# Two layers with attention on one core: loads of queries, keys and values move from SyncE's to ScalarE's DMA issue

## The chip, the core and the metric

The kernel runs on one core of a Trainium2 chip. A core has five engines with an instruction stream each: TensorE (PE in the profile, with its weight loads apart as PEld), VectorE (DVE), ScalarE (ACT), GpSimd (POOL) and SyncE (SP), which computes nothing and issues transfers. TensorE reads SBUF and writes PSUM. Transfers between DRAM and SBUF are DMAs; an engine issues one with an instruction of its own stream, and 16 DMA engines move the bytes. The engines wait for one another through semaphores only. The metric is the time of one execution on the device in microseconds, and less is better. Three runs of the kernel before gave 1760.53, 1763.01 and 1766.39 us; their median is 1763.01 us.

## The reference

Two layers work on 2 sequences of 1024 tokens with 512 features. Each layer normalizes x, computes a mixing part and a feed-forward part from it and adds both to x. The change touches the attention of the second layer alone:

```python
qkv = x @ W_qkv.T + b_qkv                       # b=2, l=1024, d=512
q, k, v = jnp.split(qkv, 3, axis=-1)            # 16 heads of 32 features
scores = jnp.einsum('bqhe,bkhe->bhqk', q, k) * scale
scores = jnp.where(causal[None, None], scores, -jnp.inf)
attn = jax.nn.softmax(scores, axis=-1)
out = jnp.einsum('bhqk,bkhe->bqhe', attn, v)
out = out.reshape(b, l, d) @ W_out.T + b_out
```

Layer 0 is a low-rank state-space mixer beside a gated feed-forward with a Walsh-Hadamard turn; layer 1 is this attention beside a gated feed-forward that keeps 2 of each 4 hidden values.

## The kernel before

The program is four phases with a barrier of all engines between them: `layer_zero`, `project_qkv`, `attention` and `layer_end`. `project_qkv` parks queries, keys and values in DRAM (`qk_parked`, `v_parked`). Every float32 operand is held as a rounded part and a rest (`hi` and `lo`), and a product is several matmuls.

`attention` takes 32 heads one after the other: 16 heads of the model times 2 sequences. `QUADS` is 4 and `HB` is 8, so a quad is 8 such heads, 4 of sequence 0 and then 4 of sequence 1. The values of one quad and one sequence lie in `v[:, b]` (1040 KB). Queries and keys of two heads (a pair) lie in one of three slots of the tile `stack` or `stack_third`.

The work of a head is this. TensorE computes 8 score blocks of 128 queries (`score`, line 1501). VectorE takes the negated maximum of each row of a block (`top`, line 1575), which gives a column of 128 numbers in `row_top`. A DMA (`place`, line 1473) writes this column as a row into the query slot, so that the second product, `turned` (line 1516), yields the transposed scores with the maximum already subtracted. Places 0 to 3 serve the first 512 queries, places 4 to 7 the second 512, and `turned` 0 and 4 wait until the four places of their half have landed (line 1509). ScalarE takes the exponential (`exp`, line 1547) and rounds it (`round`, line 1555) for 8 of 12 blocks; VectorE subtracts for those (`rest`, line 1582); GpSimd does both steps for the other 4 (`divide`, lines 1595 and 1598). TensorE multiplies by the values (`weigh`, lines 1533 and 1534) into one PSUM bank `p_o`; ScalarE reads it out twice a head (`read_o`, line 1564), which frees the bank, and SyncE stores it (`store`, lines 1480 and 1481).

The order of all this is written out by hand in the table `ORDER`, one list for each engine, which `run` walks for every head h. An entry is a step, its number within the head, and how many heads ahead of h it is. An engine executes its list strictly in this order. SyncE issues every DMA of the program. Within the attention its list holds the places, the stores, the loads of the next pair (`stack`, three DMAs of 256 KB a head, queries for even h and keys for odd h, `load_part`, line 1153) and, once each four heads, the load of values (`values`, line 1158, six of them).

Of the kernel before, what the change touches and what calls it, by code (L numbers as in the profile page):

```python
# [11 lines left out]
F32 = mybir.dt.float32  # L12
# [7 lines left out]
B, S, D = 2, 1024, 512  # L20
# [8 lines left out]
HEADS, E = 16, 32  # L29
# [1116 lines left out]
        load_part(sp, slot, qk_dram, pair, what, stacked)  # L1146


def load_part(sp, slot, qk_dram, pair, what, stacked):
    r = 2 * E * what  # L1150
    for block in range(3):
        half = block // 2 if what == 0 else block % 2
        sp.dma_start(slot[E * block:E * block + E, :, what].bitcast(F32),
                     qk_dram[pair][half, r:r + 2 * E, :].rearrange("(a e) n -> e a n", a=2)).then_inc(stacked, 16)


def load_values(sp, v, v_dram, quad, b, loaded):
    sp.dma_start(v[:, b].rearrange("p t a c -> p (t a c)").bitcast(F32), v_dram[B * quad + b]).then_inc(loaded, 16)


def project_qkv(nc, wqk, wv, masks, x_hi, x_lo, qk_dram, v_dram, stack, v_first, mask, ahead, qk_parts, qk_stored):
# [193 lines left out]
def attention(nc, mask, stack, v, qk_dram, v_dram, o_dram, sum_dram, o_both, o_stored, qk_last, load_next):  # L1355
# [3 lines left out]
    QUADS = HEADS // 4  # L1359
    HB = B * 4  # L1360
    ROWS = QB * G
    BL = 12
# [13 lines left out]
                   ("weigh", 11, 0), ("score", 4, 2), ("turned", 3, 1), ("turned", 4, 1), ("turned", 5, 1)],  # L1376
        "scalar": [("exp", 3, 0), ("exp", 4, 0), ("round", 3, 0), ("exp", 5, 0), ("round", 5, 0), ("read_o", 0, 0),
                   ("exp", 6, 0), ("exp", 7, 0), ("exp", 8, 0), ("round", 7, 0), ("exp", 9, 0), ("exp", 10, 0),
                   ("round", 9, 0), ("exp", 11, 0), ("round", 10, 0), ("round", 11, 0), ("exp", 0, 1),
                   ("round", 0, 1), ("exp", 1, 1), ("exp", 2, 1), ("round", 2, 1), ("read_o", 1, 0)],  # L1380
        "vector": [("top", 4, 1), ("rest", 2, 0), ("rest", 3, 0), ("top", 5, 1), ("rest", 5, 0), ("top", 6, 1),
                   ("rest", 7, 0), ("top", 7, 1), ("top", 0, 2), ("rest", 9, 0), ("top", 1, 2), ("top", 2, 2),
                   ("rest", 10, 0), ("rest", 11, 0), ("rest", 0, 1), ("top", 3, 2)],
        "gpsimd": [("divide", 4, 0), ("divide", 6, 0), ("divide", 8, 0), ("divide", 1, 1)],
        "sync": [("place", 4, 1), ("store", 0, 0), ("values", 0, 0), ("place", 5, 1), ("place", 6, 1), ("place", 7, 1),
                 ("stack", 2, 0), ("place", 0, 2), ("place", 1, 2), ("place", 2, 2), ("place", 3, 2), ("store", 1, 0)],
    }

    with ExitStack() as ctx:
# [9 lines left out]
        slots = [stack[:, 0], stack[:, 1], third[:]]  # L1399

        stacked = [sem(f"stacked{i}") for i in range(3)]
# [8 lines left out]
        def wait(engine, semaphore, count):  # L1410

            if count > 0:
                engine.wait_ge(semaphore, count)
# [28 lines left out]
        def run(steps, order):  # L1442
            for h in range(-AHEAD, HB * QUADS):
                for step, n, ahead in order:
                    if 0 <= h + ahead < HB * QUADS:
                        steps[step](h + ahead, n)
# [2 lines left out]

        @block.sync  # L1450
        def _(sp):
            def next_stack(h, n):
                pair = h // 2 + n
                if pair < HEADS:
                    wait(sp, turned, 2 * BL * (pair - 2))
                    load_part(sp, slots[pair % 3], qk_dram, pair, h % 2, stacked[pair % 3])
                if h == HB * (QUADS - 1):
                    load_next(sp)

            def next_values(h, n):  # L1460
                quad, at = divmod(h, HB)
                if at == 0 and quad:
                    sp.wait_ge(weighted, HB * BL * quad)
                    load_values(sp, v, v_dram, quad, 1, v_loaded[1])
                if at == 4 and quad + 1 < QUADS:
                    sp.wait_ge(weighted, HB * BL * quad + HB * BL // 2)
                    load_values(sp, v, v_dram, quad + 1, 0, v_loaded[0])

            def place(h, r):
                sp.wait_ge(topped, ROWS * h + r + 1)  # L1470
                if r % QB == 0:
                    wait(sp, placed[r // QB], 16 * QB * h)
                sp.dma_start(slot_of(h)[K3:K3 + 1, h % 2, 0, r * P:(r + 1) * P].bitcast(F32),
                             top[:, h % 2, r:r + 1].bitcast(F32)).then_inc(placed[r // QB], 16)

            def store(h, g):
                b, pr, a = place_of(h)
                sp.wait_ge(o_read, G * h + g + 1)
                row, t0, i = E * (2 * pr + a), b * S + g * W, (G * h + g) % OS
                sp.dma_start(o_dram[h // HB, :, row:row + E, t0:t0 + W], o_both[0:2 * E, i]).then_inc(o_stored[i], 16)  # L1480
                sp.dma_start(sum_dram[TT * (h // HB) + G * b + g, row // E:row // E + 1], o_both[2 * E:VC, i])\
                    .then_inc(o_stored[i], 16)

            sp.wait_ge(*qk_last)
            run({"stack": next_stack, "values": next_values, "place": place, "store": store}, ORDER["sync"])

        @block.tensor
        def _(pe):
# [51 lines left out]
        def _(act):  # L1540
# [16 lines left out]
            def read_o(h, g):  # L1557
                act.wait_ge(weighted, BL * h + (BL if g else QB))

                if (h, g) == (0, 0):  # L1560
                    act.wait_ge(*qk_last)
                i = (G * h + g) % OS
                wait(act, o_stored[i], 32 * ((G * h + g) // OS))
                act.activation(o_both[:, i], p_o[0:VC, :], ACT.Copy).then_inc(o_read, 1)

            run({"exp": exp, "round": round_block, "read_o": read_o}, ORDER["scalar"])

        @block.vector
        def _(dve):
# [555 lines left out]
```

## Time and profile before

| | |
|---|---|
| median of 3 runs | 1763.01 us |
| the profiled execution's own time | 1764.99 us |
| its span, first to last instruction | 1763.2 us |
| PE busy | 1673.1 us (95%) |
| DVE busy | 1016.8 us (58%) |
| ACT busy | 655.6 us (37%) |
| POOL busy | 559.3 us (32%) |
| mean granted TensorE clock | 0.975 of 2.4 GHz |
| DMA traffic | 141.80 MB, mean 80 GB/s |

The page divides the span into 40 slices of 44 us. The attention fills slices 18 to 27, from about 770 to 1185 us. Shares over the whole span therefore say little of it; the views by window do. Instructions that only issue a DMA are not counted as busy on their engine; the timeline shows them with a q behind the engine's name (SPq).

### The profile page before, as it was taken

The numbers are of one execution on the slowest core, as the hardware profiler recorded it, in microseconds if no ns is written. First come the engines' busy times: TensorE is split into PE (matmuls) and PEld (weight loads), VectorE is DVE, ScalarE is ACT, GpSimd is POOL, SyncE is SP. The second block draws the span as 40 slices with busy tenths as digits, with TensorE's granted clock in tenths as the row PEclk, the third lists the DMA queues.
The fourth block names the chain that finished last, engine by engine and source line by source line (L and its number), as shares of the span: only waits on it lengthen the run. The fifth ranks groups of instructions, "written<-read, shape, count | busy, mean of one in ns | idle before, by whom it ended". The sixth has DMA issues, their size and how long they took to land. (4 is left out here: it accounts for less than half of the span.)

```text
span 1763.2 us, 21900 instructions
## 1 busy us (share of the span) xinstructions
PE 1673.1 (95%) x7804; PEld 1304.7 (74%) x7804; DVE 1016.8 (58%) x1667; ACT 655.6 (37%) x1271; POOL 559.3 (32%) x540
## 2 busy tenths in 40 slices
PE   5999999999999989999888889889999999999998
PEld 3677888788788878866555556558888888888887
DVE  4321465465524452559877779774565654655785
ACT  4421322232213332248767678772222222222221
POOL 4201210310310121227666567674144031033230
PEclk9999999999999999989999899999999999999999
DMA  7200110110101139735444454415010010012243
GB/s 283 99 12 1 61 48 19 54 49 12 48 7 36 48 132 271 265 122 116 93 100 100 99 115 113 105 31 172 1 51 25 1 48 24 1 49 56 89 131 131
DMA packets 101916, 141.80 MB, mean 80 GB/s; under 512 B 43881, under 2 KB 52713, under 8 KB 100274
## 3 DMA queue, kind: packets, MB, share of 16 engines
q1 hardware_dynamic: 101810, 140.45, 27.3%
q8 instruction: 60, 0.98, 0.2%
q14 instruction: 46, 0.38, 0.1%
HBM read 93.74 MB, written 46.53 MB: 80 GB/s over the span
## 5 line engine op out<-in xcount | busy, mean ns | idle before, releaser
L1582 DVE TENSOR_TENSOR pt_lo<-prob,pt_hi 128x512 fp32r<-128x512 f32 (+3 forms) x256 | 174.3, 703 | 58.9 <-ACT pt_hi L1555 58.3
L1547 ACT ACTIVATE prob<-p_turn 128x512 f32<-128x512 f32 (+3 forms) x384 | 176.5, 487 | 74.8 <-PE p_turn L1516 44.4
L1575 DVE TENSOR_REDUCE row_top<-p_score 128x1 fp32r<-128x128 f32 (+7 forms) x256 | 183.9, 745 | 16.5 <-PE p_score L1503 15.4
L1598 POOL TENSOR_TENSOR pt_lo<-prob,pt_hi 128x512 fp32r<-128x512 f32 (+1 forms) x128 | 170.6, 1333 | 10.7
L1025 DVE TENSOR_TENSOR hid<-hid,p_up 128x512 f32<-128x512 f32 x64 | 44.0, 687 | 219.1 <-PE p_up L490 203.4
L1929 DVE TENSOR_TENSOR e_hid<-e_hid,e_p_up 128x512 f32<-128x512 f32 x64 | 44.0, 687 | 198.6 <-PE e_p_up L1824 198.6
L1533 PE MATMUL p_o<-pt_hi,v 128*65 128x512 f32 (+3 forms) x384 | 141.9, 372 | 5.1 <-POOL pt_lo L1598 2.3
L1595 POOL TENSOR_SCALAR pt_hi<-prob 128x512 fp32r<-128x512 f32 (+1 forms) x128 | 97.9, 765 | 132.3 <-ACT prob L1547 90.5
L1534 PE MATMUL p_o<-pt_lo,v 128*65 128x512 f32 (+3 forms) x384 | 132.4, 351 | 0.0
L1555 ACT ACTIVATE pt_hi<-prob 128x512 fp32r<-128x512 f32 (+3 forms) x256 | 120.6, 486 | 3.0
L772 ACT ACTIVATE hid<-p_gate 128x512 f32<-128x512 f32 x64 | 38.3, 599 | 219.7 <-PE p_gate L490 219.6
L1516 PE MATMUL p_turn<-stack 97*128 97x512 f32 (+3 forms) x264 | 93.2, 416 | 25.3 <-DMA stack<-row_top 25.3
L1872 ACT ACTIVATE mag<-e_hid 128x512 f32<-128x512 f32 x64 | 40.5, 632 | 186.0 <-DVE e_hid L1929 186.0
L326 POOL TENSOR_SCALAR gu_hi<-raw 128x512 fp32r<-128x512 f32 x32 | 23.0, 718 | 266.8 <-PE p_up L490 221.8
L488 PE MATMUL p_gate<-x_hi,gu_hi 128*128 128x512 f32 x256 | 103.0, 402 | 3.8 <-DVE x_lo L918 3.8
L1822 PE MATMUL e_p_gate<-x_hi,e_gu_hi 128*128 128x512 f32 x256 | 100.7, 393 | 4.7 <-POOL e_gu_lo L1777 4.7
L488 PE MATMUL p_up<-x_hi,gu_hi 128*128 128x512 f32 x256 | 101.9, 398 | 0.0
L501 PE MATMUL p_job<-d_hi,h_hi 128*128 128x512 f32 x256 | 100.4, 392 | 0.5 <-DVE res L1041 0.5
L490 PE MATMUL p_gate<-x_hi,gu_lo 128*128 128x512 f32 x256 | 100.6, 393 | 0.0
L1823 PE MATMUL e_p_gate<-x_lo,e_gu_hi 128*128 128x512 f32 x256 | 100.5, 393 | 0.0
L1824 PE MATMUL e_p_gate<-x_hi,e_gu_lo 128*128 128x512 f32 x256 | 100.5, 393 | 0.0
L489 PE MATMUL p_gate<-x_lo,gu_hi 128*128 128x512 f32 x256 | 100.4, 392 | 0.0
(279 smaller groups left out, 4269.5 us busy)
## 6 DMA issues: line engine op xcount, KB each, us to landing
stack<-qk_parked SPq DMA_DIRECT2D x66, 256.0 KB, 5.1
raw<-in_wgu SPq DMA_DIRECT2D x64, 256.0 KB, 2.8
qk_parked<-qk SPq DMA_DIRECT2D x16, 1024.0 KB, 4.0
v_parked<-v_out SPq DMA_DIRECT2D x16, 520.0 KB, 7.5
v<-v_parked SPq DMA_DIRECT2D x8, 1040.0 KB, 10.9
o_parked<-o_both SPq DMA_DIRECT2D x64, 128.0 KB
stack_third<-qk_parked SPq DMA_DIRECT2D x30, 256.0 KB, 4.6
res<-in_x SPq DMA_DIRECT2D x8, 512.0 KB
```

Source lines behind the costliest of these rows:

```text
L488: pe.matmul(acc[:, c % 2], gu_hi[:, c, j, k], x_hi[:, t, k], start=(k == 0), stop=False)
L490: mm = pe.matmul(acc[:, c % 2], gu_lo[:, c, j, k], x_hi[:, t, k], start=False, stop=(k == KD - 1))
L1533: pe.matmul(p_o[0:VC, c0:W], lhs, pt_hi[:, slot, c0:W], start=(kb == 0), stop=False)
L1534: pe.matmul(p_o[0:VC, c0:W], lhs, pt_lo[:, slot, c0:W], start=False, stop=(j in (QB - 1, BL - 1))).then_inc(weighted, 1)
L1547: act.activation(prob[:, n % PB, c0:W], p_turn[:, n % TB, c0:W], ACT.Exp).then_inc(exped, 1)
L1555: act.activation(pt_hi[:, n % PT, c0:W], prob[:, n % PB, c0:W], ACT.Copy).then_inc(rounded, 1)
L1575: dve.tensor_reduce(top[:, h % 2, r:r + 1], p_score[:, r % 2, 0:width_of(r)], AX_X, ALU.max, negate=True).then_inc(topped, 1)
L1582: dve.tensor_tensor(pt_lo[:, n % PT, c0:W], prob[:, n % PB, c0:W], pt_hi[:, n % PT, c0:W].bitcast(F32), ALU.subtract).then_inc(split, 1)
L1598: pool.tensor_tensor(pt_lo[:, n % PT, c0:W], prob[:, n % PB, c0:W], pt_hi[:, n % PT, c0:W].bitcast(F32), ALU.subtract).then_inc(own_split, 1)
L1822: pe.matmul(acc[:, c % 2], gu_hi[:, c, j, k], x_hi[:, x, k], start=(k == 0), stop=False)
L1823: pe.matmul(acc[:, c % 2], gu_hi[:, c, j, k], x_lo[:, x, k], start=False, stop=False)
L1824: mm = pe.matmul(acc[:, c % 2], gu_lo[:, c, j, k], x_hi[:, x, k], start=False, stop=(k == KD - 1))
```

## The change

`load_part` and `load_values` take the engine that issues as an argument. SyncE's list loses ("values", 0, 0) and ("stack", 2, 0); in the place of the latter stands ("blocks", 0, 0), which issues the first weight blocks of the next phase at head 24, as before. ScalarE's list gets ("stack", 2, 0) between `exp` 11 and `round` 10, with the wait for `turned` that SyncE had, and at head 0 a wait for the last store of queries and keys. The loads of values are issued by ScalarE behind `read_o` of the second half of heads 3 and 7 of a quad; before, SyncE issued them in heads 4 and 0, with a wait for `weighted` that `read_o` already includes. The bytes, tiles and semaphores stay as they are.

```diff
--- before.py
+++ after.py
@@ -1146,16 +1146,16 @@
         load_part(sp, slot, qk_dram, pair, what, stacked)
 
 
-def load_part(sp, slot, qk_dram, pair, what, stacked):
+def load_part(engine, slot, qk_dram, pair, what, stacked):
     r = 2 * E * what
     for block in range(3):
         half = block // 2 if what == 0 else block % 2
-        sp.dma_start(slot[E * block:E * block + E, :, what].bitcast(F32),
+        engine.dma_start(slot[E * block:E * block + E, :, what].bitcast(F32),
                      qk_dram[pair][half, r:r + 2 * E, :].rearrange("(a e) n -> e a n", a=2)).then_inc(stacked, 16)
 
 
-def load_values(sp, v, v_dram, quad, b, loaded):
-    sp.dma_start(v[:, b].rearrange("p t a c -> p (t a c)").bitcast(F32), v_dram[B * quad + b]).then_inc(loaded, 16)
+def load_values(engine, v, v_dram, quad, b, loaded):
+    engine.dma_start(v[:, b].rearrange("p t a c -> p (t a c)").bitcast(F32), v_dram[B * quad + b]).then_inc(loaded, 16)
 
 
 def project_qkv(nc, wqk, wv, masks, x_hi, x_lo, qk_dram, v_dram, stack, v_first, mask, ahead, qk_parts, qk_stored):
@@ -1376,14 +1376,14 @@
                    ("weigh", 11, 0), ("score", 4, 2), ("turned", 3, 1), ("turned", 4, 1), ("turned", 5, 1)],
         "scalar": [("exp", 3, 0), ("exp", 4, 0), ("round", 3, 0), ("exp", 5, 0), ("round", 5, 0), ("read_o", 0, 0),
                    ("exp", 6, 0), ("exp", 7, 0), ("exp", 8, 0), ("round", 7, 0), ("exp", 9, 0), ("exp", 10, 0),
-                   ("round", 9, 0), ("exp", 11, 0), ("round", 10, 0), ("round", 11, 0), ("exp", 0, 1),
+                   ("round", 9, 0), ("exp", 11, 0), ("stack", 2, 0), ("round", 10, 0), ("round", 11, 0), ("exp", 0, 1),
                    ("round", 0, 1), ("exp", 1, 1), ("exp", 2, 1), ("round", 2, 1), ("read_o", 1, 0)],
         "vector": [("top", 4, 1), ("rest", 2, 0), ("rest", 3, 0), ("top", 5, 1), ("rest", 5, 0), ("top", 6, 1),
                    ("rest", 7, 0), ("top", 7, 1), ("top", 0, 2), ("rest", 9, 0), ("top", 1, 2), ("top", 2, 2),
                    ("rest", 10, 0), ("rest", 11, 0), ("rest", 0, 1), ("top", 3, 2)],
         "gpsimd": [("divide", 4, 0), ("divide", 6, 0), ("divide", 8, 0), ("divide", 1, 1)],
-        "sync": [("place", 4, 1), ("store", 0, 0), ("values", 0, 0), ("place", 5, 1), ("place", 6, 1), ("place", 7, 1),
-                 ("stack", 2, 0), ("place", 0, 2), ("place", 1, 2), ("place", 2, 2), ("place", 3, 2), ("store", 1, 0)],
+        "sync": [("place", 4, 1), ("store", 0, 0), ("place", 5, 1), ("place", 6, 1), ("place", 7, 1),
+                 ("blocks", 0, 0), ("place", 0, 2), ("place", 1, 2), ("place", 2, 2), ("place", 3, 2), ("store", 1, 0)],
     }
 
     with ExitStack() as ctx:
@@ -1449,22 +1449,9 @@
 
         @block.sync
         def _(sp):
-            def next_stack(h, n):
-                pair = h // 2 + n
-                if pair < HEADS:
-                    wait(sp, turned, 2 * BL * (pair - 2))
-                    load_part(sp, slots[pair % 3], qk_dram, pair, h % 2, stacked[pair % 3])
+            def first_blocks(h, n):
                 if h == HB * (QUADS - 1):
                     load_next(sp)
-
-            def next_values(h, n):
-                quad, at = divmod(h, HB)
-                if at == 0 and quad:
-                    sp.wait_ge(weighted, HB * BL * quad)
-                    load_values(sp, v, v_dram, quad, 1, v_loaded[1])
-                if at == 4 and quad + 1 < QUADS:
-                    sp.wait_ge(weighted, HB * BL * quad + HB * BL // 2)
-                    load_values(sp, v, v_dram, quad + 1, 0, v_loaded[0])
 
             def place(h, r):
                 sp.wait_ge(topped, ROWS * h + r + 1)
@@ -1482,7 +1469,7 @@
                     .then_inc(o_stored[i], 16)
 
             sp.wait_ge(*qk_last)
-            run({"stack": next_stack, "values": next_values, "place": place, "store": store}, ORDER["sync"])
+            run({"blocks": first_blocks, "place": place, "store": store}, ORDER["sync"])
 
         @block.tensor
         def _(pe):
@@ -1562,8 +1549,20 @@
                 i = (G * h + g) % OS
                 wait(act, o_stored[i], 32 * ((G * h + g) // OS))
                 act.activation(o_both[:, i], p_o[0:VC, :], ACT.Copy).then_inc(o_read, 1)
-
-            run({"exp": exp, "round": round_block, "read_o": read_o}, ORDER["scalar"])
+                quad, at = divmod(h, HB)
+                if g and at % 4 == 3 and quad + 1 < QUADS:
+
+                    load_values(act, v, v_dram, quad + 1, at // 4, v_loaded[at // 4])
+
+            def next_stack(h, n):
+                pair = h // 2 + n
+                if pair < HEADS:
+                    if h == 0:
+                        act.wait_ge(*qk_last)
+                    wait(act, turned, 2 * BL * (pair - 2))
+                    load_part(act, slots[pair % 3], qk_dram, pair, h % 2, stacked[pair % 3])
+
+            run({"exp": exp, "round": round_block, "read_o": read_o, "stack": next_stack}, ORDER["scalar"])
 
         @block.vector
         def _(dve):
```

The following rows are the order of SyncE's DMAs around the first of the six loads of values, in head 4 of the first quad. `row_top` is the column of maxima, `stack` and `stack_third` the query and key slots, `o_parked` and `sum_parked` the stored results, `v` the values. Before:

```order
L1480 DMA o_parked<-o_both 2x32x512
L1481 DMA sum_parked<-o_both 1x512
L1473 DMA stack_third<-row_top 1x128x1
L1480 DMA o_parked<-o_both 2x32x512
L1481 DMA sum_parked<-o_both 1x512
L1158 DMA v<-v_parked 128x2080
L1473 DMA stack_third<-row_top 1x128x1 x3
L1153 DMA stack<-qk_parked 32x2x1024 x3
L1473 DMA stack<-row_top 1x128x1 x4
```

The same place of SyncE's list now (its lines stand 13 lower, L1460 for L1473):

```order
L1467 DMA o_parked<-o_both 2x32x512
L1468 DMA sum_parked<-o_both 1x512
L1460 DMA stack_third<-row_top 1x128x1
L1467 DMA o_parked<-o_both 2x32x512
L1468 DMA sum_parked<-o_both 1x512
L1460 DMA stack_third<-row_top 1x128x1 x3
```

The load of values and the three loads of the next pair are gone, and the last three places of a head follow the store directly.

ScalarE's instructions in the same stretch, from the last exponentials of a head to `read_o` of its second half (now also to the first step of the next head). `prob` is the exponential, `pt_hi` its rounding, `o_both` the result that is read out. Before:

```order
L1547 ACTIVATE prob<-p_turn 128x384
L1547 ACTIVATE prob<-p_turn 128x256
L1555 ACTIVATE pt_hi<-prob 128x384
L1547 ACTIVATE prob<-p_turn 128x128
L1555 ACTIVATE pt_hi<-prob 128x256
L1555 ACTIVATE pt_hi<-prob 128x128
L1547 ACTIVATE prob<-p_turn 128x512
L1555 ACTIVATE pt_hi<-prob 128x512
L1547 ACTIVATE prob<-p_turn 128x384
L1547 ACTIVATE prob<-p_turn 128x256
L1555 ACTIVATE pt_hi<-prob 128x256
L1564 ACTIVATE o_both<-p_o 65x512
```

And now:

```order
L1534 ACTIVATE prob<-p_turn 128x128
L1153 DMA stack<-qk_parked 32x2x1024 x3
L1542 ACTIVATE pt_hi<-prob 128x256
L1542 ACTIVATE pt_hi<-prob 128x128
L1534 ACTIVATE prob<-p_turn 128x512
L1542 ACTIVATE pt_hi<-prob 128x512
L1534 ACTIVATE prob<-p_turn 128x384
L1534 ACTIVATE prob<-p_turn 128x256
L1542 ACTIVATE pt_hi<-prob 128x256
L1551 ACTIVATE o_both<-p_o 65x512
L1158 DMA v<-v_parked 128x2080
L1534 ACTIVATE prob<-p_turn 128x128
```

Three issues stand ahead of the rounding of blocks 10 and 11 in each of heads 0 to 27, and one issue behind the read-out in six heads. ScalarE's list gains 28 x 3 + 6 = 90 DMAs, and SyncE's loses them.

## Rows read from the trace of the kernel before

**Rows 1.** Timeline of PE, 860 to 1110 us: start, length, engine, line, count, [idle before <-releaser].

```profile
844.02 1.22 PE L1516 MATMUL p_turn<-stack_third 97*128 97x512 f32 x2 [4.78 <-DMA stack_third<-row_top]
...
867.62 0.73 PE L1516 MATMUL p_turn<-stack 97*128 97x512 f32 x2 [0.20 <-DMA stack<-row_top]
...
894.66 0.80 PE L1516 MATMUL p_turn<-stack 97*128 97x512 f32 x1 [5.01 <-DMA stack<-row_top]
...
947.52 1.22 PE L1516 MATMUL p_turn<-stack 97*128 97x512 f32 x2 [5.79 <-DMA stack<-row_top]
...
1001.69 1.22 PE L1516 MATMUL p_turn<-stack_third 97*128 97x512 f32 x2 [5.84 <-DMA stack_third<-row_top]
...
1054.12 1.22 PE L1516 MATMUL p_turn<-stack 97*128 97x512 f32 x2 [5.42 <-DMA stack<-row_top]
...
1105.79 1.22 PE L1516 MATMUL p_turn<-stack 97*128 97x512 f32 x2 [4.59 <-DMA stack<-row_top]
```

**Rows 2.** Timeline of SP, 832 to 838 us.

```profile
832.30 0.36 SPq L1158 DMA_DIRECT2D v<-v_parked  x1
...
835.51 0.47 SPq L1473 DMA_DIRECT2D stack_third<-row_top  x1
836.02 1.53 SPq L1153 DMA_DIRECT2D stack<-qk_parked  x3
```

**Rows 3.** Line 1473, landing of all places, of that at 835.5, of that at 863.7.

```profile
DMA to landing us min/median/max: 1.9/4.3/9.6
...
DMA to landing us min/median/max: 8.5/8.5/8.5
...
DMA to landing us min/median/max: 3.9/3.9/3.9
```

**Rows 4.** The page's DMA issues: count, KB each, median us from issue to landing.

```profile
stack<-qk_parked SPq DMA_DIRECT2D x66, 256.0 KB, 5.1
...
v<-v_parked SPq DMA_DIRECT2D x8, 1040.0 KB, 10.9
```

**Rows 5.** Windows: length, busy PE PEld DVE ACT POOL, granted clock, DMA share, GB/s.

```profile
837.60:854.80 17.20, 12.36 (x66) 8.15 (x64) 10.35 (x17) 9.46 (x22) 8.34 (x9) 0.90 0.34 70
854.80:888.00 33.20, 32.82 (x194) 21.48 (x192) 31.87 (x49) 28.37 (x68) 25.52 (x25) 1.00 0.53 125
888.00:906.80 18.80, 13.67 (x72) 9.06 (x71) 11.46 (x19) 9.92 (x24) 9.35 (x10) 0.82 0.36 83
...
940.10:959.80 19.70, 13.85 (x71) 9.35 (x70) 10.86 (x20) 9.94 (x23) 8.63 (x9) 0.83 0.34 74
...
994.20:1014.00 19.80, 13.89 (x69) 9.22 (x68) 10.70 (x19) 9.98 (x24) 8.46 (x9) 0.74 0.32 66
...
1047.10:1065.70 18.60, 13.12 (x68) 8.87 (x67) 10.49 (x19) 9.57 (x23) 8.39 (x9) 0.82 0.37 74
...
1101.50:1117.00 15.50, 11.21 (x54) 7.66 (x54) 8.44 (x14) 8.19 (x20) 6.43 (x8) 0.78 0.51 115
```

**Rows 6.** Windows of the same view behind the first long wait and ahead of it.

```profile
844.00:846.00 2.00, 1.98 (x5) 1.28 (x6) 0.32 (x1) 1.14 (x3) 0.46 (x1) 0.50 0.17 45
...
836.00:840.00 4.00, 3.19 (x21) 2.04 (x20) 4.00 (x8) 2.83 (x7) 2.44 (x3) 1.00 0.85 205
```

**Rows 7.** Timeline of ACT, 862 to 869 us, an undisturbed head.

```profile
862.10 0.77 ACT L1547 ACTIVATE prob<-p_turn 128x384 f32<-128x384 f32 x2 [0.66 <-PE p_turn L1519]
...
863.16 0.28 ACT L1547 ACTIVATE prob<-p_turn 128x128 f32<-128x128 f32 x1
863.32 0.63 ACT L1555 ACTIVATE pt_hi<-prob 128x256 fp32r<-128x256 f32 x2
...
866.85 0.59 ACT L1564 ACTIVATE o_both<-p_o 65x512 f32<-65x512 f32 x1 [0.65 <-PE p_o L1534]
...
868.15 0.60 ACT L1547 ACTIVATE prob<-p_turn 128x512 f32<-128x512 f32 x1 [0.42 <-PE p_turn L1516]
```

**Rows 8.** Timeline of SP, 904 us: the slowest group of three loads.

```profile
904.12 2.65 SPq L1153 DMA_DIRECT2D stack<-qk_parked  x3
```

## The prediction

> **What bounds the kernel now.** I went from the page to the attention, because the change touches nothing else, and there I read four views: PE's timeline for its waits, SP's timeline for what was issued ahead of each, the windows of single heads, and ACT's timeline for the room in which the moved issues would stand. In PE's timeline the reader sees one pattern: six waits of about 5 us, one for each load of values, and all of them of `turned` for the column of maxima that `place` writes [rows 1]. They sum to 4.78 + 5.01 + 5.79 + 5.84 + 5.42 + 4.59 = 31.4 us. Ahead of the first stands the load of values at 832.30, then the last place of the head at 835.51, then three loads of the next pair [rows 2]. That last place needs 8.5 us to land, which is 844.0, the moment at which PE goes on; in a head without such a load it needs 3.9 us [rows 3]. The values themselves land after 10.9 us, at 843.2 [rows 4]. So a transfer of 512 bytes stands in SyncE's queue behind one of 1040 KB.
>
> The wait costs more than itself. Behind it the granted clock is 0.50, the lower level of 1.2 GHz, while PE had done nothing for 4.78 us [rows 6], and the pipeline of four engines has to fill again. The windows give the whole price. Three undisturbed heads take 33.20 us, 11.07 each. The six heads with a load of values take 17.20 + 18.80 + 19.70 + 19.80 + 18.60 + 15.50 = 109.6 us [rows 5], and six undisturbed ones would take 66.4. The excess is 43.2 us. That is all that the change can win from the values.
>
> Undisturbed heads are tight. PE is busy for 32.82 of 33.20 us, DVE for 31.87, ACT for 28.37 [rows 5]. The last place is just in time there as well: issued at 863.7 and landed 3.9 later, it is waited for by PE for 0.20 us [rows 1, 3]. A loop runs from `turned` 4 through exponentials, rounding, VectorE's subtraction and maxima to the last place and back, and the landing time of that place is a link of it. Anything that it loses, every head loses.
>
> **What goes.** SyncE no longer issues values or pairs. Its places have only stores ahead of them in its queue. If order in the queue is what held them, the 43.2 us go. I don't count all: the values still use the same DMA engines, whose share is 0.85 in the stretch after the load [rows 6]. What remains per load lies between 0 and the whole, 7.2 us (43.2/6). I take 1.2 us, nearer to the 0.20 of a head without the load than to a full wait, so 6 x 1.2 = 7.2 us stay, and 36.0 go. ScalarE also issues the values some 3 us earlier, behind `read_o` instead of behind the next head's first store, which helps the same way.
>
> **What is added.** ScalarE issues 3 DMAs in each of heads 0 to 27. On SP a group of three takes 1.53 us [rows 2] and 2.65 at worst [rows 8]. The trace shows no DMA issued by ACT, so the price is bounded: 0 if ScalarE computes while its issue runs, 2.65 a head at the other end; I take 1.53, because most of SP's groups cost that. The exponential in front starts at 863.16 and the rounding behind it at 863.32 [rows 7]; with 1.53 between, the rounding starts about 1.5 us later. Behind it wait blocks 10 and 11, then an exponential and a rounding of the next head, then `read_o`. `read_o` waits 0.65 for PE today and absorbs that much, so 0.85 is left. The next exponential with a wait has 0.42, which leaves 0.43, and the one at 862.10 has 0.66 in which the rest ends [rows 7]. Over a head ACT has 11.07 - 9.46 = 1.61 us idle, so 1.53 just fits. What PE loses is what falls between the first and the last of these waits: `weigh` 0 needs the bank that `read_o` frees, and GpSimd's block 4 needs the exponential. That is 0 to 0.85 us; I take the middle, 0.4, and 28 x 0.4 = 11.2 us. The six issues of values, 0.36 us each [rows 2], follow `read_o` in the heads that had the long wait and lie inside the 1.2. The semaphore waits that move along are met long before (the `turned` of the previous pair ended a head ago), and cost nothing. SyncE saves 1.53 us of issue a head, but its last place is issued as soon as its maximum is there, so that wins nothing.
>
> **The sum**, against the profiled execution's own 1765.0 us: 1765.0 - 36.0 + 11.2 = 1740.2. The median of the runs shown lies 2.0 lower, so the forecast is 1738 us, taken as 1739.
>
> The Trainium skill has a sentence that bears on this. In "DMA: Bandwidth & Descriptors", section "Issuing engines are not separate DMA queues", it says that DMAs from scalar, sync and gpsimd run on the same 16 engines and interleave, and that issuing from several engines saves only the sequencer's time. Read strictly, the change would save nothing of the wait, as SP's time to issue isn't what PE waits for. The same page, section "Queues, rings and completion order", gives SP and ACT a ring each on every DMA engine, served in turns, and by that a place would pass the values. The 8.5 against 3.9 us fits both, since in the trace everything stands in one queue.
>
> **Rivals.**
> First, the engines are what holds the place, not the order. The values keep the DMA engines occupied from whichever queue they come; only their earlier issue helps. For it speaks the share of 0.85; against it that a place of 512 bytes needs little of any engine. Half of the excess stays, and 1765.0 - 21.6 + 11.2 = 1754.6, or 1753 on the scale of the runs.
>
> Second, slower. Today the three loads of the next pair stand behind the last place in one queue (835.51, then 836.02) and can't overtake it [rows 2]. From ScalarE they are issued at about 863.4, while the last place goes out at 863.7, and the two queues compete. A load of a pair takes 5.1 us to land [rows 4], a place between 1.9 and 9.6 [rows 3]. If the last place lands 1.3 us later in each of 28 heads (a third of the way from 3.9 to the 8.5 that it has beside the values), the loop grows by as much: 36.4 us. It would come with half of the excess staying, as it is the same contention: 1765.0 - 21.6 + 36.4 = 1779.8, or 1778. It decides from 0.8 us a head on if half of the excess goes (21.6/28), and from 1.3 if 36.0 go. ScalarE's issue at its dear end, 2.65 with 1.61 idle, would give 1.04 a head and point the same way.
>
> Third, both effects cancel within 5 us: 1763.
>
> Fourth, ScalarE's issue is free and all of the excess but 7.2 us goes: 1765.0 - 36.0 = 1729.0, or 1727.
>
> **Chances.** Forecast 0.40; issue free 0.06; engines hold the place 0.18; cancel 0.09; slower 0.27. About 0.3% (5 us) is what a measurement of this kernel can tell from no change. The case of half the excess at 1753 lies mostly below that bound, so 0.12 of its 0.18 count as faster. Faster: 0.40 + 0.06 + 0.12 = 0.58. Same: 0.09 + 0.06 = 0.15. Slower: 0.27. The range of the likeliest case alone is 1727 to 1750: at the low end nothing stays of the wait beside a cost of 0.4 a head (1765.0 - 43.2 + 11.2 - 2.0 = 1731) or the issue is free; at the high end the cost is 0.8 a head. The range for 8 in 10 has to reach into both other signs: 1720, a little below the free issue with nothing left of the waits (1765.0 - 43.2 - 2.0 = 1720), to 1784, past the slower case.
>
> **What would show it.** Right: PE's six long waits for `row_top` are under 2 us each, no granted clock near 0.5 within the stage, heads of 11.3 to 11.6 us, ACT issues of about 0.5 us each, and the last place landing in 4 us or less also beside the values. Engines hold: waits of 2 to 4 us at the same six places. Slower: short waits of `turned` for `row_top` of 1 us or more in nearly every head, and last places that land 5 us or more after their issue. If instead ACT's waits for PE have gone and PE waits for `o_both` or for POOL's `pt_lo`, the issue time was the cost. The forecast is wrong if heads without a load of values take over 12 us.

## The result, and the profile after

The changed kernel takes 1830.88 us (median of 4 runs, 1823.42 to 1835.06) beside 1761.77 us for the kernel before on the same chip: a ratio of 1.0378, with a 95% interval of 1.0352 to 1.0404. It is slower by about 69 us, and lies outside the forecast range.

The page of the profile after, first the busy times, then the issues with count, KB each and median us to landing:

```profile
span 1833.2 us, 21900 instructions
PE 1701.0 (93%) x7804; PEld 1329.3 (73%) x7804; DVE 1001.6 (55%) x1667; ACT 654.3 (36%) x1271; POOL 540.4 (29%) x540
...
L1503 PE MATMUL p_turn<-stack 97*128 97x512 f32 (+3 forms) x264 | 104.2, 456 | 54.4 <-DMA stack<-row_top 54.4
...
stack<-qk_parked ACTq DMA_DIRECT2D x54, 256.0 KB, 4.2
...
v<-v_parked ACTq DMA_DIRECT2D x6, 1040.0 KB, 6.4
```

The instructions are as many as before and ScalarE's busy time has hardly changed. PE is 27.9 us longer busy with the same 7804 matmuls. The values land in 6.4 us instead of 10.9 [rows 4]. So the loads have moved and themselves go faster, and the kernel is slower.

PE's timeline after, six of its waits for a place, which answer to [rows 1]:

```profile
797.67 1.22 PE L1503 MATMUL p_turn<-stack 97*128 97x512 f32 x2 [3.12 <-DMA stack<-row_top]
813.38 1.22 PE L1503 MATMUL p_turn<-stack 97*128 97x512 f32 x2 [2.60 <-DMA stack<-row_top]
828.76 0.72 PE L1503 MATMUL p_turn<-stack 97*128 97x512 f32 x2 [3.20 <-DMA stack<-row_top]
843.51 0.84 PE L1503 MATMUL p_turn<-stack_third 97*128 97x512 f32 x2 [2.68 <-DMA stack_third<-row_top]
859.07 1.22 PE L1503 MATMUL p_turn<-stack_third 97*128 97x512 f32 x2 [3.45 <-DMA stack_third<-row_top]
...
905.38 1.22 PE L1503 MATMUL p_turn<-stack 97*128 97x512 f32 x2 [2.99 <-DMA stack<-row_top]
```

The six waits of about 5 us are gone. In their place stands one of about 3 us in nearly every head, also in heads without values. The one at 905.38, behind a load of values (issued at 902.18), is no longer than its neighbours. All waits of `turned` for places:

```profile
  PE p_turn L1503: 79.9, 29
```

Before, the same sum was 36.4 us in 15 waits. What happens in one head is seen in ScalarE's timeline, then SyncE's, then the landing of the place at 852.16:

```profile
850.73 0.77 ACT L1534 ACTIVATE prob<-p_turn 128x384 f32<-128x384 f32 x2 [0.65 <-PE p_turn L1506]
851.35 0.32 ACTq L1153 DMA_DIRECT2D stack<-qk_parked  x1
851.38 0.53 ACT L1542 ACTIVATE pt_hi<-prob 128x384 fp32r<-128x384 f32 x1
851.70 0.45 ACTq L1153 DMA_DIRECT2D stack<-qk_parked  x1
851.80 0.28 ACT L1534 ACTIVATE prob<-p_turn 128x128 f32<-128x128 f32 x1
852.18 0.45 ACTq L1153 DMA_DIRECT2D stack<-qk_parked  x1
852.73 0.62 ACT L1542 ACTIVATE pt_hi<-prob 128x256 fp32r<-128x256 f32 x2 [0.65 <-ACT prob L1534]
```

```profile
852.16 0.47 SPq L1460 DMA_DIRECT2D stack_third<-row_top  x1
```

```profile
DMA to landing us min/median/max: 6.9/6.9/6.9
```

The last place of the head goes out at 852.16, between the second and the third load of the pair, and lands 6.9 us later, at 859.1, when PE goes on. The four places of a half share one semaphore, and the view counts landings on it in the order of issue. So the landing of the last place is the moment at which all four have landed, which is what `turned` waits for. In the undisturbed head before it took 3.9 [rows 3], with the pair's loads issued behind it in the same queue: [rows 2] show that order, 0.51 us apart. Now the first load of the pair goes out 0.4 to 1.0 us ahead of the last place, in all 28 heads that load one, and the last places of these heads land after 4.5 to 7.5 us. The difference of 3.0 us in this head is about the wait of 3.45. ScalarE pays little: the issues begin ahead of the last exponential and run beside it, and 0.65 us of idle time remain ahead of the rounding, where [rows 7] has none.

Windows of the head behind the wait that ends at 859.07, and of two stretches of 2 us, the first around the end of that wait (columns as in [rows 5]):

```profile
860.30:876.10 15.80, 13.04 (x65) 8.86 (x65) 9.83 (x16) 9.43 (x23) 7.63 (x8) 0.82 0.32 67
859.00:861.00 2.00, 1.93 (x5) 1.24 (x6) 0.27 (x1) 1.10 (x3) 0.41 (x1) 0.50 0.17 48
861.00:863.00 2.00, 2.00 (x10) 1.60 (x9) 0.75 (x2) 0.82 (x2) 1.48 (x2) 0.50 0.01 3
```

This head takes 15.8 us, where an undisturbed one took 11.07. Behind the wait the granted clock is 0.50, as it was in the first 2 us behind each of the six waits before ([rows 6] show the first), but now it happens in most heads: behind 26 of the 29 waits it is 0.50 to 0.54 in one of the two stretches of 2 us that follow.

The account can be drawn up for the attention alone, from its first `score` matmul to the first matmul of the last phase. Before, then after:

```profile
769.93:1189.32 419.39, 371.63 (x2049) 244.72 (x2049) 338.87 (x512) 305.08 (x706) 271.18 (x260) 0.92 0.41 94
```

```profile
770.21:1260.85 490.64, 401.38 (x2049) 270.83 (x2049) 322.60 (x512) 304.06 (x706) 252.33 (x260) 0.85 0.36 80
```

It is 71.2 us longer. PE is busy 29.8 us longer with as many matmuls, at a mean granted clock of 0.85 instead of 0.92, and idle 41.5 us longer. The waits for places are 79.9 - 36.4 = 43.5 us more, so its other idle time is 2.0 us less. That all of the 29.8 us is the lower clock is not shown: in e10_early_split below PE is also longer busy, at an undiminished clock.

### The profile page after: what moved, and what is told of

Read it like the earlier page. It is cut to its first block and busy times, and to the rows that moved or that the text cites. A ratio compares the mean times of both kernels' runs of the same rounds, so it can differ in the third digit from the quotient of the medians.

```text
span 1833.2 us, 21900 instructions
## 1 busy us (share of the span) xinstructions
PE 1701.0 (93%) x7804; PEld 1329.3 (73%) x7804; DVE 1001.6 (55%) x1667; ACT 654.3 (36%) x1271; POOL 540.4 (29%) x540
## 5 line engine op out<-in xcount | busy, mean ns | idle before, releaser
L1581 DVE TENSOR_TENSOR pt_lo<-prob,pt_hi 128x512 fp32r<-128x512 f32 (+3 forms) x256 | 155.0, 620 | 121.3 <-ACT pt_hi L1542 121.1
L1597 POOL TENSOR_TENSOR pt_lo<-prob,pt_hi 128x512 fp32r<-128x512 f32 (+1 forms) x128 | 161.0, 1257 | 10.7
L1503 PE MATMUL p_turn<-stack 97*128 97x512 f32 (+3 forms) x264 | 104.2, 456 | 54.4 <-DMA stack<-row_top 54.4
L1594 POOL TENSOR_SCALAR pt_hi<-prob 128x512 fp32r<-128x512 f32 (+1 forms) x128 | 88.7, 693 | 223.4 <-ACT prob L1534 176.8
L1520 PE MATMUL p_o<-pt_hi,v 128*65 128x512 f32 (+3 forms) x384 | 148.0, 390 | 4.6 <-POOL pt_lo L1597 2.3
L1521 PE MATMUL p_o<-pt_lo,v 128*65 128x512 f32 (+3 forms) x384 | 137.6, 374 | 0.0
L490 PE MATMUL p_up<-x_hi,gu_lo 128*128 128x512 f32 x256 | 99.9, 390 | 0.0
```

The costliest lines, as they stand in the source:

```text
L1503: mm = pe.matmul(to[:, c0:W], both[:, 1, kb * P:(kb + 1) * P], both[:, 0, g * W + c0:(g + 1) * W], start=True, stop=kb < QB * g)
L1520: pe.matmul(p_o[0:VC, c0:W], lhs, pt_hi[:, slot, c0:W], start=(kb == 0), stop=False)
L1521: pe.matmul(p_o[0:VC, c0:W], lhs, pt_lo[:, slot, c0:W], start=False, stop=(j in (QB - 1, BL - 1))).then_inc(weighted, 1)
L1581: dve.tensor_tensor(pt_lo[:, n % PT, c0:W], prob[:, n % PB, c0:W], pt_hi[:, n % PT, c0:W].bitcast(F32), ALU.subtract).then_inc(split, 1)
L1597: pool.tensor_tensor(pt_lo[:, n % PT, c0:W], prob[:, n % PB, c0:W], pt_hi[:, n % PT, c0:W].bitcast(F32), ALU.subtract).then_inc(own_split, 1)
```

## The experiments

Theory A: the pair's loads, in a second queue beside the last place, share the DMA engines with it and make it late. Theory B: ScalarE's time to issue is what costs. Theory C: it is the values in the second queue. Theories D and E concern the shape of the store. All ratios are to the kernel before on the same chip.

**Values alone from ScalarE (e1_values).** The pairs stay in SyncE's queue.

```diff
-            def first_blocks(h, n):
+            def next_stack(h, n):
+                pair = h // 2 + n
+                if pair < HEADS:
+                    wait(sp, turned, 2 * BL * (pair - 2))
+                    load_part(sp, slots[pair % 3], qk_dram, pair, h % 2, stacked[pair % 3])
```

> Only the six loads of values are issued by ScalarE; the pairs stay behind the last place in SyncE's queue. Theory A (the pairs' loads, issued in a second queue beside the last place of a head, share the DMA engines with it and let it land at 6.9 us instead of 3.9): heads without values return to 11.1 us, and the six waits of about 5 us shrink because values now start some 3 us earlier in the other queue: 1725 to 1745 us. Theory B (what costs is ScalarE's time to issue 84 loads): the same heads, the same range, so this run does not part A from B. Theory C (it is the values in the other queue that harm): 1800 us or more, with the waits of 3 us in all heads.

1740.48 us, ratio 0.9871 (0.9839 to 0.9902). This half of the change alone wins 22 us. Theory C falls. PE still waits for places, 22.6 us in 20 waits, the first behind a load of values:

```profile
842.42 0.49 PE L1507 MATMUL p_turn<-stack_third 97*128 97x512 f32 x1 [1.82 <-DMA stack_third<-row_top]
```

This is not the wait of [rows 1] in a shorter form. It stands ahead of `turned` 0, and so for the first four places of the head; `turned` 4 goes on at 845.98 without a wait. ScalarE's row, then SyncE's, then the landing of the fourth place, issued at 833.88:

```profile
833.09 0.34 ACTq L1158 DMA_DIRECT2D v<-v_parked  x1
```

```profile
832.06 2.41 SPq L1464 DMA_DIRECT2D stack_third<-row_top  x4
```

```profile
DMA to landing us min/median/max: 8.5/8.5/8.5
```

The values are in the other queue, and the four places have landed only at 842.4, 0.3 us behind the values (842.0). It is so at all six loads: 0.3 to 0.6 us behind them here, 0.5 to 0.8 us in the kernel before, where all stood in one queue. So the other queue does not let the places by. What has changed is the moment: the last place, which in an undisturbed head is just in time [rows 1, 3], goes out 7.8 us behind the first load of values instead of 3.2, and lands in 4.8 us instead of 8.5.

**Pairs alone from ScalarE (e2_pairs).** `next_values` is back in SyncE's list, and the call behind `read_o` is gone.

> Only the pairs' loads are issued by ScalarE; values stay in SyncE's queue. Theory A and B: the wait of about 3 us for the last place stays in each of 28 heads, and the six heads with values keep a wait of 5 us or more: 1830 to 1850 us. Theory C: near 1765 us.

1856.12 us, ratio 1.0536 (1.0502 to 1.0570), 6 us above the expected range. The wait of about 3 us is in most heads, and that behind the first values is longer than before (4.78):

```profile
811.96 0.73 PE L1512 MATMUL p_turn<-stack 97*128 97x512 f32 x2 [2.76 <-DMA stack<-row_top]
...
856.27 1.22 PE L1512 MATMUL p_turn<-stack_third 97*128 97x512 f32 x2 [6.88 <-DMA stack_third<-row_top]
```

So the two halves have opposite signs: values -22 us, pairs +94.

**The same issues 3.5 us later (e3_late).**

```diff
-                   ("round", 9, 0), ("exp", 11, 0), ("stack", 2, 0), ("round", 10, 0), ("round", 11, 0), ("exp", 0, 1),
-                   ("round", 0, 1), ("exp", 1, 1), ("exp", 2, 1), ("round", 2, 1), ("read_o", 1, 0)],
+                   ("round", 9, 0), ("exp", 11, 0), ("round", 10, 0), ("round", 11, 0), ("exp", 0, 1),
+                   ("round", 0, 1), ("exp", 1, 1), ("exp", 2, 1), ("round", 2, 1), ("read_o", 1, 0), ("stack", 2, 0)],
```

> As the changed kernel, but ScalarE issues the three loads of a pair at the end of a head's list, behind the read-out of its second half, about 3.5 us later; the number of issues on ScalarE is the same. Theory A: the last place has gone by when the pair's data move and lands in about 4 us; heads of 11.1 to 11.8 us, 1725 to 1755 us. Theory B: ScalarE loses the same time per head, and more of it stands directly ahead of the exponential that PE waits for: 1820 us or more.

1758.24 us, ratio 0.9971 (0.9956 to 0.9986): 73 us better than the changed kernel with the same issues on the same engine. Theory B can't explain the 69 us. It missed the range of theory A by 3 us, and the timelines show two waits that go with the new place of the issue. ScalarE now stands idle behind the issue, and behind the six loads of values the pair lands late and PE waits for it in `score`, 2.0 to 3.2 us each time:

```profile
884.98 0.28 ACT L1534 ACTIVATE prob<-p_turn 128x128 f32<-128x128 f32 x1 [1.70 <-DVE pt_lo L1581]
```

```profile
892.02 0.33 PE L1488 MATMUL p_score<-stack_third 96*128 96x128 f32 x1 [2.22 <-DMA stack_third<-qk_parked]
```

The first row puts 1.70 us down to a releaser, but the issue of the three loads (883.09, 1.79 us) fills that gap.

**The last place from ScalarE too, ahead of the pair (e4_last).**

```diff
-                   ("round", 9, 0), ("exp", 11, 0), ("stack", 2, 0), ("round", 10, 0), ("round", 11, 0), ("exp", 0, 1),
+                   ("round", 9, 0), ("exp", 11, 0), ("last", 7, 1), ("stack", 2, 0), ("round", 10, 0), ("round", 11, 0), ("exp", 0, 1),
...
-        "sync": [("place", 4, 1), ("store", 0, 0), ("place", 5, 1), ("place", 6, 1), ("place", 7, 1),
+        "sync": [("place", 4, 1), ("store", 0, 0), ("place", 5, 1), ("place", 6, 1),
...
+            def last_place(h, r):
+                act.wait_ge(topped, ROWS * h + r + 1)
+                act.dma_start(slot_of(h)[K3:K3 + 1, h % 2, 0, r * P:(r + 1) * P].bitcast(F32),
+                              top[:, h % 2, r:r + 1].bitcast(F32)).then_inc(placed[r // QB], 16)
```

> As the changed kernel, but ScalarE also issues the last place of a head, directly ahead of the pair's loads, so that the two stand in one queue in the old order. Theory A in the form that the turn-taking between two queues is what delays the last place: it lands in 4 us or less again although the pair's loads start at the same moment as in the changed kernel; 1730 to 1760 us. If instead the pair's loads slow any transfer that runs at that moment, whatever its queue: landing stays at 6 to 7 us and the time at 1815 to 1835 us. Theory B: one issue more on ScalarE, slower than 1831 us.

1784.48 us, ratio 1.0115 (1.0069 to 1.0160). The expectation of the time failed, but the landing came out as theory A has it. The landing of the 32 places issued by ScalarE, and the timeline of one head:

```profile
DMA to landing us min/median/max: 1.9/2.6/7.0
```

```profile
881.36 0.48 ACTq L1567 DMA_DIRECT2D stack<-row_top  x1
881.87 1.57 ACTq L1153 DMA_DIRECT2D stack_third<-qk_parked  x3
883.54 0.61 ACT L1542 ACTIVATE pt_hi<-prob 128x256 fp32r<-128x256 f32 x2 [2.42 <-PE p_o L1521]
```

Ahead of the pair in its own queue the place lands in 2.6 us, with the pair's data right behind it, and PE's waits for places fall to 3.5 us in 3. But ScalarE now waits for the maximum, its issues no longer run beside an exponential, and it stands idle for 2.42 us in such a head. The releaser in the row had long been done; the two rows above it fill the time. So ScalarE's issue does cost where nothing covers it. The run changes two things about the place, though: its queue, and its moment, since it now goes out 0.52 us ahead of the first load of the pair instead of 0.4 to 1.0 us behind it. Which of the two brings the landing down, it can't tell.

**The kernel before with a split store (e5_split_before).** The store's outer dimension was 2; now two transfers of 32 rows, with 48 for 32 in the counts of `o_stored`.

```diff
-                sp.dma_start(o_dram[h // HB, :, row:row + E, t0:t0 + W], o_both[0:2 * E, i]).then_inc(o_stored[i], 16)
+                for half in range(2):
+                    sp.dma_start(o_dram[h // HB, half, row:row + E, t0:t0 + W], o_both[E * half:E * half + E, i])\
+                        .then_inc(o_stored[i], 16)
```

> The kernel before with each 128 KB store of results as two transfers of 32 partitions instead of one whose outer dimension is 2. Theory D (the last place of a head lands at 3.9 instead of 1.9 us because a store of this shape, ahead of it, keeps few DMA engines busy for long): the last places land in about 2.5 us, the short waits of 0.2 to 1.2 us go, the six long waits shrink by 1 to 2 us each: 1740 to 1755 us. Theory E (the store's shape has no part in it): 1763 us, or a little more for 64 issues more of 0.5 us on SyncE.

1721.76 us, ratio 0.9757 (0.9724 to 0.9789), more than was expected. The queue and its order are those of the kernel before, values and all:

```profile
v<-v_parked SPq DMA_DIRECT2D x8, 1040.0 KB, 5.9
```

```profile
838.13 0.73 PE L1518 MATMUL p_turn<-stack_third 97*128 97x512 f32 x2 [1.11 <-DMA stack_third<-row_top]
```

The values land in 5.9 us instead of 10.9, and the long wait is 1.11 instead of 4.78 [rows 1, 4]. The last places behind the six loads of values land after 3.8 to 5.4 us instead of 8.3 to 9.6. So it was not the 1040 KB ahead of the place alone that made most of the six long waits, but the values and the place behind stores of this shape. The Trainium skill, in "DMA: Bandwidth & Descriptors", section "Why a DMA increments its semaphore by 16 and not by 1", says that the number of DMA engines of a transfer is the largest up to 16 that divides the outer dimension on both sides. By that rule the store ran on 2 engines and its halves on 16. The landing times fit this; no view here shows the engines one by one.

**The changed kernel with a split store (e6_split_after).** The same edit on the changed kernel.

> The changed kernel with the split store. Theory A with D (the last place is late because the pairs' loads in the second queue take turns with the stores and the place, and most on the few engines that the stores load): landing falls from 6.9 to about 4 us, heads to 11.5 to 12.5 us, 1740 to 1780 us. Theory A with E: the place still stands beside the pairs' packets, 1820 to 1835 us.

1821.88 us, ratio 1.0312 (1.0277 to 1.0347). The waits for places are 69.4 us in 28, hardly fewer than 79.9. The stores explain the waits of before and not those of after: the place stands beside the pair's data whatever the stores do.

**Values from ScalarE and a split store (e7_values_split).** The edits of e1_values and e5_split_before together.

> Values from ScalarE, pairs from SyncE, split store: the run of values alone (1740 us) with the split store. Theory D: the 22.6 us of waits for places that were left there go for the most part: 1715 to 1730 us. Theory E: 1740 us or slightly more.

1719.60 us, ratio 0.9751 (0.9715 to 0.9787), the best median, but not told apart from e5_split_before. With the stores spread, the queue of the values no longer matters.

**Without the pairs' loads (e8_no_pairs).**

```diff
                     wait(act, turned, 2 * BL * (pair - 2))
-                    load_part(act, slots[pair % 3], qk_dram, pair, h % 2, stacked[pair % 3])
+                    if pair < 3:
+                        load_part(act, slots[pair % 3], qk_dram, pair, h % 2, stacked[pair % 3])
```

> The changed kernel without the loads of pairs 3 to 15; queries and keys of the first three pairs are used again, so the output is not the reference's. Values still come from ScalarE. Theory A: with nothing beside it the last place lands in about 4 us or less, the waits of 3 us go, 1725 to 1740 us. If the waits of 3 us stay, the pairs' loads are not what delays the place: 1800 us or more.

1723.82 us, ratio 0.9766 (0.9733 to 0.9799), 1 us below the expected range. The first two heads still load pair 2, and the trace holds both cases:

```profile
795.43 0.73 PE L1503 MATMUL p_turn<-stack 97*128 97x512 f32 x2 [3.25 <-DMA stack<-row_top]
810.43 1.22 PE L1503 MATMUL p_turn<-stack 97*128 97x512 f32 x2 [2.74 <-DMA stack<-row_top]
890.47 0.73 PE L1503 MATMUL p_turn<-stack 97*128 97x512 f32 x2 [0.92 <-DMA stack<-row_top]
```

Beside a pair's load the wait is 3.25 and 2.74 us. Without it the next wait comes 80 us later and is 0.92.

**Half the bytes (e9_half), and next to none (e11_tiny).** `load_part` takes a width n; for pairs from 3 on it is `S // 2` or 16 tokens. The number of transfers and of rows stays.

```diff
-        engine.dma_start(slot[E * block:E * block + E, :, what].bitcast(F32),
-                     qk_dram[pair][half, r:r + 2 * E, :].rearrange("(a e) n -> e a n", a=2)).then_inc(stacked, 16)
+        engine.dma_start(slot[E * block:E * block + E, :, what, 0:n].bitcast(F32),
+                     qk_dram[pair][half, r:r + 2 * E, 0:n].rearrange("(a e) n -> e a n", a=2)).then_inc(stacked, 16)
```

> The changed kernel with half the tokens in each load of pairs 3 to 15: as many DMAs and as many rows as before, each of half the bytes; the other half of each slot keeps old data, so the output is not the reference's. Theory A with turn-taking (each of a place's small packets waits for one packet of the pair's loads, so the delay follows the time of a packet): waits of about 3 us shrink to 0.5 to 1.5 us each, 1745 to 1785 us. If the delay follows the number of packets and not their size, or has another cause: 1815 to 1831 us.

> The changed kernel with only 16 tokens in each load of pairs 3 to 15: the 84 DMAs are issued by ScalarE at the same place and have as many rows, but carry 64 bytes a row instead of 4096 (so the output is not the reference's). What is left above the run without these loads (1724 us) is ScalarE's time to issue. Theory B in what is left of it: 0.4 to 1.5 us a head, 1735 to 1765 us. Theory A alone, with the issues hidden behind the exponentials: 1722 to 1732 us.

Half: 1745.32 us, ratio 0.9889 (0.9856 to 0.9923), waits for places 27.3 us in 24. Tiny: 1728.31 us, ratio 0.9821 (0.9798 to 0.9844), 14.0 us in 15. With 4096, 2048, 64 and no bytes a row the medians are 1831, 1745, 1728 and 1724 us. The places land after 4.3, 3.1, 2.8 and 2.7 us in the median (those into `stack`). The time grows with the bytes and faster than in proportion: the second half of the bytes costs 86 us, the first 17. Between the profiled executions of the changed kernel and of the half (93.7 us) PE's waits for places differ by 52.6 us and its busy time, with the same matmuls, by 42.3 (1701.0 and 1658.7); between the half and the tiny loads (13.6 us) only the waits do, by 13.3. The mean granted clock of the three is 0.954, 0.986 and 0.983: the second half of the bytes also brings the lower clock, and the first does not.

Between the tiny loads and none lie 4.5 us in the medians (9.7 by the ratios, whose intervals touch). That bounds ScalarE's time for the 78 issues in 26 heads by which the two runs differ: 0.2 to 0.4 us a head. ScalarE stands idle for 0.65 us ahead of the rounding in most heads of e9_half and e11_tiny, just as in the changed kernel, so that idle time is not what the 69 us are made of.

**The issues 4.5 us earlier, with a split store (e10_early_split).**

```diff
-                   ("exp", 6, 0), ("exp", 7, 0), ("exp", 8, 0), ("round", 7, 0), ("exp", 9, 0), ("exp", 10, 0),
-                   ("round", 9, 0), ("exp", 11, 0), ("stack", 2, 0), ("round", 10, 0), ("round", 11, 0), ("exp", 0, 1),
+                   ("stack", 2, 0), ("exp", 6, 0), ("exp", 7, 0), ("exp", 8, 0), ("round", 7, 0), ("exp", 9, 0), ("exp", 10, 0),
+                   ("round", 9, 0), ("exp", 11, 0), ("round", 10, 0), ("round", 11, 0), ("exp", 0, 1),
```

The edit of the store is that of e6_split_after.

> The changed kernel with the three issues on ScalarE moved about 4.5 us ahead, between the read-out of the first half and exponential 6, and with the split store. Theory A: the pair's data have gone by when the last place is issued; it lands in about 3 us, no waits of 3 us. ScalarE pays for the issue here, because a full exponential stands behind it: up to 1.5 us a head. 1715 to 1760 us. If the place of the issue did not matter, as in the run with the split store alone: 1815 to 1825 us.

1764.68 us, ratio 0.9995 (0.9979 to 1.0011), 5 us above the expected range. The DMA view and ScalarE's timeline:

```profile
stack<-row_top SPq DMA_DIRECT2D x176, 0.5 KB, 2.0
```

```profile
892.81 1.41 ACTq L1153 DMA_DIRECT2D stack<-qk_parked  x3
894.32 1.09 ACT L1536 ACTIVATE prob<-p_turn 128x512 f32<-128x512 f32 x2 [0.92 <-PE p_turn L1508]
```

The places land in 2.0 us in the median and PE never waits for one. The loads and their queue are those of e6_split_after, only their moment differs: theory A holds once more. The partner for what is left is e7_values_split, from which this run differs only in who issues the pairs and when: by the ratios it is 43 us slower, 1.5 us for each of 28 heads. ScalarE is idle for about 1 us behind the issue in each head (the issue at 892.81 fills the gap that the row puts down to PE), and PE waits 35.8 us for `pt_lo`, which needs ScalarE's exponentials. That points at theory B for this place of the issue; PE's busy time also grew, by 20.2 us (1678.8 and 1658.6), at nearly the same granted clock (0.985 and 0.988), and that is not explained.

## Why the prediction was wrong

**The step that failed** is the price of the pairs' loads beside the last place. The forecast's own sum put nothing on it; only the second rival did, and with it too little. The prediction named the place (loads of the pair issued at 863.4 beside a last place at 863.7, in two queues), the loop that passes it on, and the point from which it decides. It put 1.3 us a head on it, called a third of the way between two landing times; a third of the 4.6 us between 3.9 and 8.5 would have been 1.5. The run of values alone stands at 1740.5 and the changed kernel at 1830.9, so moving the pairs cost 90.4 us, 3.2 a head. The last place landed 3.0 us later in the head shown, two thirds of the way. Between the profiled executions of these two kernels (95.2 us) PE's waits for places differ by 57.3 us (79.9 and 22.6), 2.0 a head, and its busy time by 37.0 us (1701.0 and 1664.0) with the same matmuls, at a mean granted clock of 0.954 instead of 0.985. For the second part the sum had no term. The prediction knew the row of the lower clock, but used it only for the waits that were to go.

**Values: sign right, mechanism wrong.** The sum let 36.0 us go, on the ground that order in the queue held the places. Measured alone it was 22 us, and e1_values shows the places landing just behind the values from the other queue too. What helped is that the values are issued earlier beside the last place. The prediction had that as an aside, and as the whole of its first rival, with half of the excess (21.6 us) staying and half going; that 22 us went is that figure, but the half was a guess from no row. The greater part of the waits hung on the stores: the same order with a spread store wins 43 us. In [rows 3] the last place took 3.9 us even without values, twice its minimum of 1.9; that was the hint at the stores, and the prediction passed over it.

**ScalarE's issue: 11.2 us forecast, 4.5 to 9.7 measured** as its upper bounds. The reasoning assumed that the rounding would start 1.5 us later; it started 0.65 late, because the issues run beside the exponentials. The size was near, by the share that was taken as absorbed, and that is luck rather than the reasoning. The dear end shows where a wait or no work stands in front of the issue: 2.42 us idle in e4_last, up to 1.5 a head in e10_early_split.

**Heads of 11.3 to 11.6 us** were to be seen, and the one above took 15.8. The sign given for the slower case, waits of 1 us or more in nearly every head and last places landing 5 us or later, is what the trace shows. The other sign, PE waiting for `o_both`, does not appear.

The Trainium skill, in "DMA: Bandwidth & Descriptors", section "Queues, rings and completion order", has each DMA engine serve the rings in turns, and the prediction took that as a way for the place to pass the values. The trace of e1_values does not bear this use out (8.5 us to landing). Serving in turns cuts both ways: the place had been ahead of the pair in one queue, and in turns it shares with it. The landing of 6.9 us beside 2.6 in e4_last, and the fall with the bytes of a row in e9_half and e11_tiny, would fit that. They would also fit a place that simply stands behind loads issued 0.4 to 1.0 us before it, whatever the queue. In the changed kernel the third load goes out 0.3 us or more behind the last place in five heads, and the place lands there after 4.5, 4.6, 5.9, 6.3 and 6.5 us, so the moment counts for something and does not settle it. No run issues the pair from ScalarE 0.5 us behind a last place that stays with SyncE, so the share of the queue and that of the order stay open.

## What to carry to other kernels

When a small transfer is what a loop waits for, ask of each bulk transfer how long before or behind it it is issued. One engine's list fixes that order by itself: here the pair stood 0.51 us behind the last place. Moved to a second engine's list, nothing keeps the bulk behind, and the pair went out 0.4 to 1.0 us ahead. Moving the values won because they then went out earlier beside the last place; moving the pairs lost because they then went out before it, and issuing the same pairs 3.5 us later took the loss back. And before moving anything look at the landing time of the critical transfer in a quiet stretch: if it is twice its minimum, something else is in its way, and here the shape of a store was worth twice what the better half of the change was.

## What the runs showed of the hardware that was not expected

- ScalarE issues DMAs beside its own work. In the changed kernel the first issue starts at 851.35 and the exponential ahead of it in the list at 851.80; three issues cost 0.65 us of idle time. With a wait for another engine ahead of them they cost 2.42.
- A store of 128 KB as one transfer with outer dimension 2, or as two of 32 rows, changes the landing of a load of 1040 KB in the same queue from 10.9 to 5.9 us, at the price of 64 more issues.
- A load of 1040 KB delays small transfers of another queue too: places of 0.5 KB issued by SyncE up to 1.4 us behind values that ScalarE issued (e1_values) land after 5.7 to 8.6 us.
- Waits of 1.7 to 4.1 us on PE, 26 of them in the changed kernel, were each followed by a granted clock of 0.50 to 0.54 within 4 us; behind the three waits of 0.8 to 0.9 us it stayed at 1.00. It can fall late: behind the wait of 3.20 us the pair of matmuls at 828.76 still runs in 0.72 us, and the windows show the fall 2 us later:

```profile
828.76:830.76 2.00, 2.00 (x10) 1.36 (x11) 0.61 (x1) 1.43 (x4) 0.70 (x2) 0.89 0.16 47
830.76:832.76 2.00, 2.00 (x11) 1.49 (x9) 1.55 (x2) 1.62 (x3) 1.20 (x1) 0.50 0.01 4
```
